# Keys and values ahead of the queries, and a one-hot product for the first block, in a perceiver layer

## What is computed

```python
x = x + xattn(layernorm(x), ctx, ctx)      # 16 heads of 32; softmax over 1601 keys; Wq, Wk, Wv, Wo with biases
x = x + attn(layernorm(x))                 # its value width is HD - ROPE = 0: it adds nothing
logits = layernorm(x) @ router_w + router_b          # 8 experts, the best 2 of each token
gates = softmax(logits of the two kept, others -1e30)
h = relu(xn @ w1[e] + b1[e]); y = h @ w2[e] + b2[e]  # 512 -> 2048 -> 512 for each expert
x = x + sum over e of gates[:, e] * y[e]
```

## Time and profile before

| | us |
|---|---|
| runs (three) | 1179.09, 1180.70, 1180.71; median 1180.70 |
| profiled execution | 1179.54 |
| its span, first to last instruction | 1177.8 |
| mean granted TensorE clock | 0.987 of full |

### The profile page before, as it was taken

One profiled execution on the slowest core, in us unless ns is written; L12 is line 12 of the kernel. 1 busy time (PEld: TensorE's weight loads), 2 busy tenths in 40 slices (PEclk: granted clock), 3 DMA queues, 4 the chain that ended last, 5 costly groups with the idle time before them and its releaser, 6 DMA issues.

```text
span 1177.8 us, 25041 instructions
## 1 busy us (share of the span) xinstructions
PE 1135.2 (96%) x8090; PEld 1083.1 (92%) x8090; DVE 984.3 (84%) x2290; ACT 725.5 (62%) x1499; POOL 495.8 (42%) x429
## 2 busy tenths in 40 slices
PE   4899999999999999999999999998999999999996
PEld 4799999999999999999999999975899999999995
DVE  6568888888888989888888888878788888888885
ACT  3455665656566565655656565633577677777774
POOL 6356555556647556565655555220112011111111
PEclk9899999999999999999999999998899999999998
DMA  5231221212122121212212120313777887778773
GB/s 185 84 90 41 65 56 57 63 52 60 44 72 60 44 72 40 63 49 63 60 53 63 43 60 24 102 61 113 256 226 237 265 253 235 240 232 269 241 237 112
DMA packets 81643, 136.74 MB, mean 116 GB/s; under 512 B 11528, under 2 KB 36232, under 8 KB 81616
## 3 DMA queue, kind: packets, MB, share of 16 engines
q1 hardware_dynamic: 78496, 129.12, 34.0%
q0 software_dynamic: 3120, 7.28, 2.9%
HBM read 130.29 MB, written 6.09 MB: 116 GB/s over the span
## 4 chain that ended last, share of the span: by engine, by line
PE 89%; DVE 5%; ACT 3%; issue 1%; DMA 1%; DVEq 1%; POOL 0%; ACTq 0%; SPq 0%; POOLq 0%
PE ps L1544 16%; PE ps L414 13%; PE ps L416 12%; PE ps L415 12%; PE ps L1390 8%; PE ps L1447 7%; PE ps L1545 6%; PE ps L1428 5%; PE ps L1429 4%; PE ps L1537 1%; ACT y_gated L875 1%; PE ps L1580 1%; ACT w_hi L799 1%; DMA wq_raw<-in_wq_dram 1%; PE ps L1402 1%
## 5 line engine op out<-in xcount | busy, mean ns | idle before, releaser
L555 POOL TENSOR_TENSOR ctx_hi<-ctx_raw,no_query 128x1152 fp32r<-128x1152 f32 x64 | 142.8, 2232 | 290.5 <-PE ps L416 281.7
L963 DVE SCALAR_TENSOR_TENSOR k_mix<-ps,bk_sb,k_mix 64x384 fp32r<-64x384 f32 (+1 forms) x256 | 162.3, 634 | 82.4 <-ACT k_mix L716 78.1
L756 ACT ACTIVATE probs<-ps,negmax 128x1152 f32<-128x1152 f32 x64 | 78.3, 1223 | 197.1 <-DVE negmax L1045 197.1
L414 PE MATMUL ps<-wv_hi,ctx_hi 128*128 128x256 f32 (+1 forms) x624 | 181.8, 291 | 6.7 <-DVE k_mix L963 6.5
L559 POOL TENSOR_TENSOR ctx_lo<-ctx_raw,ctx_hi 128x1152 fp32r<-128x1152 f32 x64 | 179.6, 2806 | 5.0
L416 PE MATMUL ps<-wv_hi,ctx_lo 128*128 128x256 f32 (+1 forms) x624 | 175.7, 282 | 0.0
L415 PE MATMUL ps<-wv_lo,ctx_hi 128*128 128x256 f32 (+1 forms) x624 | 174.9, 280 | 0.0
L1544 PE MATMUL ps<-xg_mix,w_hi 128*128 128x320 f32 x584 | 165.6, 351 | 0.7 <-DVE h_sum L1223 0.7
L716 ACT ACTIVATE k_mix<-ps,bk_sb 64x384 fp32r<-64x384 f32 (+1 forms) x256 | 150.8, 589 | 24.1 <-PE ps L416 19.6
L1544 PE MATMUL ps<-h_mix,w_hi 128*128 128x320 f32 x576 | 161.4, 349 | 2.8 <-DVE h_mix L1229 1.9
L1058 DVE TENSOR_TENSOR pt_mix<-ps,pt_mix 128x384 fp32r<-128x384 f32 (+1 forms) x256 | 142.2, 580 | 2.4 <-ACT pt_mix L767 2.3
(11 more groups left out here) (207 smaller groups left out, 2721.7 us busy)
## 6 DMA issues: line engine op xcount, KB each, us to landing
w_raw<-in_w_dram SPq DMA_DIRECT2D x76, 1024.0 KB, 5.6
ctx_raw<-in_ctx_t_dram SPq DMA_DIRECT2D x48, 576.0 KB, 3.8
ctx_raw<-in_ctx_t_dram SPq DMA_DIRECT2D x16, 673.5 KB, 4.0
q_both<-q_scratch SPq DMA_DIRECT2D x14, 128.0 KB, 3.0
x<-in_x_dram SPq DMA_DIRECT2D x1, 1024.0 KB, 5.3
wq_raw<-in_wq_dram SPq DMA_DIRECT2D x1, 1024.0 KB, 7.5
q_scratch<-q_out SPq DMA_DIRECT2D x1, 1024.0 KB, 5.7
wo_raw<-in_wo_dram SPq DMA_DIRECT2D x1, 1024.0 KB, 5.2
```

The costliest lines, as they stand in the source:

```text
L414: pe.matmul(acc_ap, a_hi, b_hi, start=start, stop=False)
L555: nc.gpsimd.tensor_tensor(ctx_hi[slot][:, :, 0:n], ctx_raw[slot][:, :, 0:n], no_query[:].rearrange("p (o i) -> p o i", o=1).broadcast_to([ ...
L963: last = nc.vector.scalar_tensor_tensor(out=k_mix[other, 2 * a + i, cols], in0=ps[rows, bank, 0:m], scalar=bk_sb[rows, a:a + 1], in1=k_mix ...
```

## The change

- At the beginning SP loads the biases, then wk and chunk 0 of the context in three pieces each, wv, chunk 1, x and wq. The order of TensorE is chunk 0, chunk 1, turning of x, query product, chunks 2 and 3. ScalarE and VectorE split wk and chunk 0 by pieces, and ScalarE chunk 1 (high); GpSimd makes the low parts of chunk 1 (three instructions) and of wq (four).
- The normalisation of x is spread between the splits of the units; its variance plus epsilon comes from ScalarE, and one small step fewer remains. The queries' group 0 is laid out during the query product, the other groups by two copies after each unit of chunk 2 (high) and 3 (low).
- The inverse softmax sum is two reciprocals of 64 partitions that write their place directly (L1064 and L1067 before). `pv_taken` is signalled once a batch.
- In steps 5 to 7 of the last batch `take_context` sums with one input in PSUM (`alone`).
- GpSimd's passes over ot_raw and ot_lo are cut by group, and wo_lo by its four parts.
- The first block's rows come, already turned, from a plain fp32 product of xn with `sel`. `find_rows(0)` and `take_rows(0)` move behind it. The bias product has 72 rows (high, high and low gates against high, low and high b2) in one pass. acc is stored before it, ScalarE copies the product into acc, and a second DMA adds it to the output.
- Places of the first stage's tiles in memory are laid out anew. The diff below is cut: left out are declarations, the split of wk and chunk 0 by pieces, and the making of the two 72-row operands by copies and subtractions on GpSimd, ScalarE and VectorE.

```diff
+            sp.dma_start(bk_sb[:], bk_t).then_inc(bias_loaded, 16)
+            sp.dma_start(bq_sb[:], bq_t).then_inc(bias_loaded, 16)
+            sp.dma_start(bv_sb[:], bv_t).then_inc(bias_loaded, 16)
+            for k in range(KC):
+                sp.dma_start(wkv_raw[:, 0, k, :], wk[k * P:(k + 1) * P, :]).then_inc(first_loaded[k], 16)
+                sp.dma_start(ctx_raw[0][:, k, 0:KEYS[0]], ctx_view[0, :, k, 0:KEYS[0]]
+                             ).then_inc(first_loaded[k] if k < KC - 1 else ctx_loaded[0], 16)
+            sp.dma_start(wkv_raw[:, 1], wv.rearrange("(k p) n -> p k n", p=P)).then_inc(wv_loaded, 16)
+            load_ctx(0, 1, 1)
             sp.dma_start(x0[:], x_rows).then_inc(x_loaded, 16)
             sp.dma_start(wq_raw[:], wq.rearrange("(k p) n -> p k n", p=P)).then_inc(wq_loaded, 16)
-            sp.dma_start(bq_sb[:], bq_t).then_inc(bias_loaded, 16)
-            sp.dma_start(bk_sb[:], bk_t).then_inc(bias_loaded, 16)
-            sp.dma_start(bv_sb[:], bv_t).then_inc(bias_loaded, 16)
-            sp.dma_start(wkv_raw[:, 0], wk.rearrange("(k p) n -> p k n", p=P)).then_inc(wkv_loaded, 16)
-            sp.dma_start(wkv_raw[:, 1], wv.rearrange("(k p) n -> p k n", p=P)).then_inc(wkv_loaded, 16)
-            load_ctx(0, 0, 0)
-            load_ctx(0, 1, 1)
             for m in range(2, CHUNKS):
...
             make_norm_tables()
-            for m in range(CHUNKS):
-                split_ctx(m + 1, m, 16 * (m // 2 + 1), UNIT0[m - 1] if m >= 2 else None)
+            pool.wait_ge(ctx_high, 2)
+            pool.wait_ge(ctx_split, 1)
+            for k in range(KC):
+                part = nc.gpsimd.tensor_tensor(ctx_lo[1][:, k, 0:KEYS[1]], ctx_raw[1][:, k, 0:KEYS[1]],
+                                               ctx_hi[1][:, k, 0:KEYS[1]].bitcast(F32), ALU.subtract)
+            part.then_inc(ctx_split, 1)
+            pool.wait_ge(wq_high, 1)
+            for k in range(KD):
+                part = nc.gpsimd.tensor_tensor(wq_lo[:, k, :], wq_raw[:, k, :], wq_hi[:, k, :].bitcast(F32), ALU.subtract)
+            part.then_inc(wq_split, 1)
+            for m in range(2, CHUNKS):
+                split_ctx(m + 1, m, 16 * (m // 2 + 1), UNIT0[m - 1])
 
...
+            for g in range(GROUPS):
+                nc.gpsimd.tensor_tensor(ot_raw[:, g, early], ot_raw[:, g, early],
+                                        bv_sb[:, g:g + 1].broadcast_to([P, TILES_BEFORE * P]), ALU.add).then_inc(ot_biased, 1)
+                pool.wait_ge(ot_biased, g + 1)
+                nc.gpsimd.tensor_tensor(ot_lo[:, g, early], ot_raw[:, g, early], ot_hi[:, g, early].bitcast(F32),
+                                        ALU.subtract).then_inc(ot_early, 1)
             pool.wait_ge(wo_high, 1)
-            nc.gpsimd.tensor_tensor(wo_lo[:], wo_raw[:], wo_hi[:].bitcast(F32), ALU.subtract).then_inc(wo_split, 1)
+            for k in range(KD):
+                nc.gpsimd.tensor_tensor(wo_lo[:, k, :], wo_raw[:, k, :], wo_hi[:, k, :].bitcast(F32),
+                                        ALU.subtract).then_inc(wo_split, 1)
...
-            gather_rows(0)
+            pool.wait_ge(xn_ready, 2 * TT)
+            nc.gpsimd.dma_start(out_rows, acc[:]).then_inc(rows_moved, 16)
+            nc.gpsimd.memset(gates_mix[:].bitcast(F32), 0.0).then_inc(lanes_cleared, 1)
+            pool.wait_ge(rows_moved, 16)
             pool.wait_ge(y_summed, TT)
-            nc.gpsimd.dma_start(out_rows, acc[:]).then_inc(sums_stored, 16)
+            nc.gpsimd.dma_start(out_rows, acc[:], accum_op=ALU.add).then_inc(rows_moved, 16)
...
+            job_high(None, 0, range(UNITS[0]))
+            split_first(wq_raw[:], wq_hi[:], wq_loaded).then_inc(wq_high, 1)
+            job_high(None, 1, range(1))
+            act.wait_ge(var_ready, 1)
+            nc.scalar.activation(sd[:], mv[:, :, 1], ACT.Sqrt, bias=eps[:, 0:1])
+            nc.scalar.activation(ve[:], mv[:, :, 1], ACT.Identity, bias=eps[:, 0:1]).then_inc(sd_ready, 1)
+            job_high(None, 1, range(1, UNITS[1]))
+            for k in range(KD):
+                act.wait_ge(xt_ready, k + 1)
+                nc.scalar.copy(xt0_hi[:, k, :], ps[:, k, :]).then_inc(xt_high, 1)
+            warm(ACT.Exp, 1)
+            act.wait_ge(zeroed, 10)
+            act.wait_ge(q_done, 1)
+            for i in range(2 * HPG):
+                src, to, pairs, cols = first_queries(i, 0, 1)
+                last = nc.scalar.copy(qbd_hi[to, pairs, cols], q_out[src, 0:1, 0:NQ])
+            last.then_inc(qbd_high, 1)
+            act.wait_ge(q_done, KD - 1)
+            act.wait_ge(pv_taken, 1)
+            for c in range(2, CHUNKS):
+                for k in range(UNITS[c]):
+                    job_high(None, c, [k])
+                    if c == 2 and k < HPG:
+                        for i in (2 * k, 2 * k + 1):
+                            src, to, pairs, cols = first_queries(i, 1, GROUPS)
+                            last = nc.scalar.copy(qbd_hi[to, pairs, cols], q_out[src, 1:GROUPS, 0:NQ])
+            last.then_inc(qbd_high, GROUPS - 1)
...
+            def take_bias_product(t):
+
+                act.wait_ge(b2_product, t + 1)
+                nc.scalar.copy(acc[:, t, :], ps[:, t, :]).then_inc(y_summed, 1)
+
             gathered_high(0)
+            act.wait_ge(rows_moved, 16)
             act.wait_ge(b1_set, 1)
             for c in range(HIDDEN_AHEAD):
+                take_bias_product(2 * c)
                 low_term(0, c)
+                take_bias_product(2 * c + 1)
                 relu_high(0, c)
...
+            def inverse_deviation(n):
+
+                dve.wait_ge(sd_ready, n)
+                step(nc.vector.reciprocal(rs0[:], sd[:]))
+                step(nc.vector.tensor_tensor(sq[:], ve[:], rs0[:], ALU.mult))
+                step(nc.vector.tensor_tensor(sdn[:], sd[:], sq[:], ALU.add))
+                step(nc.vector.reciprocal(rs0[:], sdn[:]))
+                step(nc.vector.tensor_tensor(rstd[:], rs0[:], rs0[:], ALU.add))
+
+            def normal_rows(src, dst, tiles):
+                for t in tiles:
+                    nc.vector.tensor_scalar(dst[:, t, :], src[:, t, :], mv[:, t, 0:1], rstd[:, t:t + 1],
+                                            ALU.subtract, ALU.mult).then_inc(xn_ready, 1)
...
+                if alone:
+                    parts = 2 * (s - CHUNKS)
+                    nc.vector.tensor_reduce(pv_low[:], ps[HALF:P, PV_BANK, 0:2 * P].rearrange("p (i r) -> p r i", i=2),
+                                            AX.X, ALU.add).then_inc(pv_part, 1)
+                    dve.wait_ge(pv_part, parts + 1)
+                    nc.vector.tensor_tensor(pv_high[:], ps[0:HALF, PV_BANK, 0:P], pv_low[:], ALU.add).then_inc(pv_part, 1)
+                    dve.wait_ge(pv_part, parts + 2)
+                    for h in range(2):
+                        rows, cols = slice(HD * h, HD * (h + 1)), slice(NQ * h, NQ * (h + 1))
+                        to = HALF * (s % 2) + HD * h
+                        last = nc.vector.tensor_tensor(ot_raw[to:to + HD, s // 2, tokens_of(b)],
+                                                       ps[rows, PV_BANK, P + NQ * h:P + NQ * (h + 1)],
+                                                       pv_high[rows, cols], ALU.add)
+                    last.then_inc(pv_free, 1)
+                    return
...
+            job_low(None, 0, KEY_UNITS)
+            dve.wait_ge(x_loaded, 16)
+            for t in range(TT):
+                last = nc.vector.bn_stats(stat[:, t, :], x0[:, t, :])
+                if t < TT - 1:
+                    job_low(None, 0, [len(KEY_UNITS) + t])
+            step(last)
+            variance()
+            job_low(None, 1, KEY_UNITS[:1])
+            inverse_deviation(1)
+            job_low(None, 1, KEY_UNITS[1:])
+            normal_rows(x0, xn0, range(2))
+            job_low(None, 1, [len(KEY_UNITS)])
+            normal_rows(x0, xn0, range(2, TT))
+            job_low(None, 1, range(len(KEY_UNITS) + 1, UNITS[1]))
+            for k in range(KD):
+                dve.wait_ge(xt_high, k + 1)
+                nc.vector.tensor_tensor(xt0_lo[:, k, :], ps[:, k, :], xt0_hi[:, k, :].bitcast(F32),
+                                        ALU.subtract).then_inc(xt_split, 1)
+            for m in range(KD):
+                dve.wait_ge(q_ready, m + 1)
+                nc.vector.tensor_scalar(q_out[:, m, :], ps[:, q_bank(m), :], bq_sb[:, m:m + 1], SCALE,
+                                        ALU.add, ALU.mult).then_inc(q_done if m < KD - 1 else pv_taken, 1)
+                if m == 0:
+                    dve.wait_ge(qbd_high, 1)
+                    dve.wait_ge(zeroed, 10)
+                    for i in range(2 * HPG):
+                        src, to, pairs, cols = first_queries(i, 0, 1)
+                        last = nc.vector.tensor_tensor(qbd_lo[to, pairs, cols], q_out[src, 0:1, 0:NQ],
+                                                       qbd_hi[src, pairs, cols].bitcast(F32), ALU.subtract)
```

(58 more changed lines are left out.)

211 lines of the change are left out of this document (102 added, 109 removed).

## The result

The changed kernel takes 1188.3 us (four runs, 1188.07 to 1188.88) against 1180.7, 7.6 us slower by the medians (ratio 1.0065, 95% interval 1.0053 to 1.0078), where I had forecast 3 us faster.

A forecast was written before the change was run, and what follows sets the result against it. TensorE, busy 96% of the span, was taken as the bound. Terms +3.5 - 1.2 - 1.6 - 3.2 = -2.5 gave 1177.0 us on the profiled execution, 1177.5 from the median; forecast range 1173 to 1180.5, with rivals 1165 to 1183.

The forecast's parts named there:

- The loop: Steps between beginning and last batch: L1067 becomes a second reciprocal of some 0.07 us; gain 1.2 us.
- my bound of +1: Slow end for the loop: a loss of 1 us, with a reciprocal as dear as L1067.
- (a): Beginning, before the first scores: normal rows wait for GpSimd passes, first scores at 70.6 against 67.1; 3.5 us lost.
- The turns: Beginning: VectorE's two-SBUF-input operations and GpSimd's passes alternate by whole instructions; the last normal rows finish at 38.0.
- turn and splits: Beginning, after the normal rows: turning x and splitting it takes 5.1 us at the low clock.
- My bound of 5.5 lost: Slow end for the beginning: 5.5 us lost, with one more long wait.
- Rivals 1 and 2: Beginning: only small sums wait, 1169 us (22%); or no turn-taking that matters, 1165 us (13%).
- (b): Last batch's steps without projections: small sums and L1067 no longer wait behind GpSimd; gain 1.6 us (0.5 to 2.2).
- Both causes that I named: Last batch's long 10.0 us step: L997 held behind L617 and the first acc pass, L1067 behind the third.
- (c): Mixture's first block: one-hot products on 128 rows bring the clock back after some 5 us; gain 3.2 us (0 to 4.7).
- Rival 3: First block: clock stays low, costing the whole 3.2 us gain; +1.2 in sum, up to 1183 us; 17%.
- the slower side: Outcome slower than the kernel before: chance 0.15, explained mainly by the first block's clock staying low.

The follow-up runs named there:

- old norm back: Changed kernel with one reciprocal of 128 sums behind the first split and the product with head_of behind the second, as before the change: 1180.7 us, ratio 1.0006.
- last two stages alone: Kernel before with only the last batch's and the first block's edits, its beginning and softmax norm unchanged: 1174.5 us, ratio 0.9949.
- two reciprocals alone: Kernel before with only the two reciprocals of 64 partitions in place of the one reciprocal and the product with head_of: 1187.1 us, ratio 1.0051.

## Why the prediction was wrong

**The loop (-1.2 forecast, +6.3 measured) is the step that failed, and it failed in its sign.** I wrote that L1067 on the chain "becomes a second reciprocal of some 0.07". Three things were wrong in it. The 0.07 is right behind an instruction that starts at partition 0; the second of the pair starts at partition 64, so it and the split behind it each wait for the end of what runs: 0.16 + 0.19. The Trainium skill states this rule ("VectorE: DVE Perf Modes", "Two Vector instructions with no wait between them"), and I had not weighed it; the runs agree with it, as told above. Both stand ahead of the second split, so three banks are late, not two. And my bound of +1 took one operation "as dear as L1067", while 0.15 us more in each of 60 steps at the 70% that reaches the scores is 6. The view was there: the 9.1 us of the earlier trace rows said that this chain is exposed. I read it as room to gain, and it was as much room to lose.

**(a) The beginning (+3.5 forecast, +9.8 measured): right mechanism, too short a sum.** The turns happened as told: rows done at 39.4 (38.0), first scores at 74.5 (70.6). This agrees with the rule of the Trainium skill cited there ("SBUF — State Buffer", "Who interferes with whom"): a `tensor_scalar` of 512 columns waits whole GpSimd passes. The terms against their measures: rows 1.4 later; turn and splits 5.1 as said; the query product 13.2 instead of 11.1, because the clock that fell in the stop rose only at 48.45, where I took full clock from the product's start; chunks 2 and 3 with the query pieces 16.8 for 16.4. That is 3.9. The other 2.4 lies behind the first score: 1.8 of it is the last low part of the queries beside a GpSimd pass. I had listed these pieces as 1.3 us of extra work, without asking which pass runs beside them, though it is the same kind of operation as L945. My bound of 5.5 lost was too near for both reasons. The 2.1 of the query product is partly the luck of this trace: in four other traces with this beginning the clock rose at 42.3 to 43.1, the product took 11.3 to 11.4 us, and the first scores came at 72.0 to 72.2, 1.6 above my sum at most. Rivals 1 and 2, in which the rows don't wait, are refuted by the rows of 2.75 and 3.25 us that fell to 0.54 with the passes away.

**(b) The last batch (-1.6 forecast, -1.7 measured): right.** Step 62 takes 8.4 us like its neighbour, L1077 takes 0.44 us for two sums beside wo_lo, where L997 took 3.46. Both causes that I named are there, each with its share: with the sums cured and L1067 in place step 62 takes 9.3 us (old norm back; last two stages alone), with L1067 gone and the sums as before 9.1 (two reciprocals alone), and 10.0 before the change. So 0.9 of the 1.7 comes from the edit of the norm, on the same kernel where that edit loses 6.3 in the loop.

**(c) The first block (-3.2 forecast, -5.1 measured): right, undersized.** One-hot start, 7.1 us of it and the clock's rise 5 us in came as forecast, the rise partly by luck: with the last two stages alone it came 3.1 us in, and from the scores of step 63 to the first h_sum it was 46.1 us instead of 47.1. The first h_sum gains 4.3, for 3.5 in my sum; 0.8 more comes behind it, 0.35 by the last h_sum and 0.45 after it, where I had let ScalarE's bias copies take 0.4 back. The cause of this 0.8 stays open. Rival 3 (clock stays low) did not happen; that the time went up has another cause than the one I gave the slower side. Its sum was off too: with the 3.2 gone my own terms give +3.5 - 1.2 - 1.6 = +0.7, not +1.2. None of my rivals lay in the loop.

## To carry to other kernels

A delay of 0.15 us on a chain that each of 60 steps waits for cost 6.3 us here, more than the whole first block gained (5.1): read the idle time that the chain's waiter shows as exposure in both directions, price each form by its distance from start to start, and keep neighbours on VectorE at the same start partition. Where work on VectorE with all its operands in SBUF and GpSimd's passes overlap, order them by whose result is needed first: here a wait that left GpSimd idle for 4.2 us won 9.4. A wait must stand on the pass that collides, not on the queue's next one.

## What the hardware did that I had not expected

- A change of start partition costs a small operation more than its work: from start to start 0.07 us behind a reciprocal that starts at partition 0, 0.19 behind one that starts at 64, with durations of 0.15 and 0.16.
- The same beginning can run 2 us longer or shorter. The first scores of the unchanged one came at 67.1 (kernel before), 67.4 (three runs), and 69.1 and 69.2 (two others). The windows from 17 to 22 show why, kernel before, then the one with the two reciprocals:
```profile
17.00:22.00 5.00, 3.51 (x16) 2.64 (x16) 4.00 (x4) 3.73 (x4) 4.92 (x3) 1.00 0.08 6
```
```profile
17.00:22.00 5.00, 3.51 (x11) 2.64 (x10) 4.00 (x4) 3.92 (x4) 4.92 (x3) 1.00 0.00 0
```
  The same 3.51 us hold 16 matmuls in the one and 11 in the other: there the products of 512 columns start 0.43 us apart until 22.5 and 0.23 apart from 22.9 on. The column of the clock says 1.00 in both, but the record of the clock begins only at 17.6 in the one and 22.8 in the other, so it says nothing of the time before. The 1.00 of the earlier trace rows from 13.9 is of this kind: the 16 turning products took 3.65 us there, and 3.68 at a recorded 0.50 in the kernel after. The profiled execution of the kernel before was one of the lucky ones.
- The changed beginning varies in the same way. The clock fell at 27.9 to 29.4 in all six traces that have it without a wait, and stayed low for 20.5 us in two of them (first scores at 74.2 and 74.5, the kernel after among them) and for 13.7 us in four (72.0 to 72.2).
- How long the clock stays low in the first block varies too: 3.4 us or 6.8 in the kernels with the one-hot product first, but 13.7 and 17.1 in those with the 8-row products first.
